# Expert values in halves with a bank each, and a token phase that begins with short spans

## The reference, cut to what matters

```python
logits = x_flat @ W_router
probs = jax.nn.softmax(logits, axis=-1)
topk_p, topk_i = jax.lax.top_k(probs, TOP_K)
topk_p = topk_p / topk_p.sum(axis=-1, keepdims=True)
...
for e in range(E):
    h = jax.nn.relu(x_flat @ W1[e] + b1[e])
    y = h @ W2[e] + b2[e]
    out = out + combine[:, e:e + 1] * y
```

## Time and profile before

| | us |
|---|---|
| median of 3 runs | 1411.34 |
| range of the runs | 1411.24 to 1416.61 |
| the profiled execution, its time | 1410.25 |
| its span, first to last instruction | 1408.4 |
| first row copy of the expert loop starts at | 448.7 |
| last row copy of the expert loop starts at | 942.2 |

### The profile page before, as it was taken

One profiled execution on the slowest core, in us unless ns is written; L12 is line 12 of the kernel. 1 busy time (PEld: TensorE's weight loads), 2 busy tenths in 40 slices (PEclk: granted clock), 3 DMA queues, 4 the chain that ended last, 5 costly groups with the idle time before them and its releaser, 6 DMA issues. The chain is left out here.

```text
span 1408.4 us, 32619 instructions
## 1 busy us (share of the span) xinstructions
PE 1103.4 (78%) x9950; PEld 731.9 (52%) x9951; DVE 825.5 (59%) x1640; ACT 744.3 (53%) x1748; POOL 546.3 (39%) x401
## 2 busy tenths in 40 slices
PE   6869787665602999999999989965999999965586
PEld 2324344332302988888888888862444444422354
DVE  3653345443525555555555555542899999984576
ACT  5855397655711555555555555544666666622364
POOL 0000006555570322322322222232799999991000
PEclk9989899888755999999999999998999999985599
DMA  6100001331122111111111111112111111101000
GB/s 202 47 1 0 1 1 54 112 129 52 33 67 62 44 39 37 38 38 37 37 38 38 38 37 37 38 31 82 30 30 60 60 60 60 46 30 77 0 1 30
DMA packets 60525, 65.22 MB, mean 46 GB/s; under 512 B 9841, under 2 KB 50301, under 8 KB 60336
## 3 DMA queue, kind: packets, MB, share of 16 engines
q1 hardware_dynamic: 49616, 46.47, 11.3%
q0 software_dynamic: 8832, 17.00, 3.7%
q10 hardware_dynamic: 2016, 0.94, 0.2%
HBM read 37.12 MB, written 28.55 MB: 47 GB/s over the span
## 5 line engine op out<-in xcount | busy, mean ns | idle before, releaser
L921 DVE SCALAR_TENSOR_TENSOR m_hl<-ps,m_hh 128x512 f16<-128x512 f32 x292 | 200.4, 686 | 158.2 <-ACT m_hh L893 155.9
L801 POOL DMA_INDIRECT expert_out<-m_result,m_token x148 | 144.5, 976 | 377.8 <-DVE m_result L933 374.1
L893 ACT ACTIVATE m_hh<-ps 128x512 f16<-128x512 f32 x292 | 174.2, 596 | 179.0 <-PE ps L854 176.7
L836 PE MATMUL ps<-m_x,weights 128*128 128x128 f16 x1168 | 212.8, 221 | 44.5 <-ACT m_x L887 43.7
L838 PE MATMUL ps<-m_x,weights 128*128 128x128 f16 x1168 | 211.7, 220 | 0.0
L837 PE MATMUL ps<-m_x,weights 128*128 128x128 f16 x1168 | 211.7, 220 | 0.0
L745 POOL DMA_INDIRECT dispatched<-d_rows,slot x128 | 128.4, 1003 | 211.6 <-DVE slot L647 126.2
L851 PE MATMUL ps<-weights,m_hh 128*128 128x128 f16 x1160 | 209.2, 219 | 0.0
L853 PE MATMUL ps<-weights,m_hl 128*128 128x128 f16 x1160 | 209.2, 219 | 0.0
L852 PE MATMUL ps<-weights,m_hh 128*128 128x128 f16 x1160 | 209.2, 219 | 0.0
L1043 POOL TENSOR_TENSOR iv_pool_sum<-iv_pool_sum,iv_pool_part 128x1024 f32<-128x1024 f32 x80 | 188.6, 2358 | 12.1 <-DVE iv_pool_part L1258 3.8
(11 more groups left out here) (306 smaller groups left out, 2238.0 us busy)
## 6 DMA issues: line engine op xcount, KB each, us to landing
m_rows<-dispatched SPq DMA_DIRECT2D x152, 65.5 KB
X<-x SPq DMA_DIRECT2D x16, 512.0 KB, 4.3
iv_got<-expert_out SPq DMA_DIRECT2D x16, 512.0 KB, 4.3
out<-X SPq DMA_DIRECT2D x16, 512.0 KB, 3.0
Y<-w_moe SPq DMA_DIRECT2D x8, 512.0 KB
expert_out<-m_result,m_token POOLq DMA_INDIRECT x148, 2.2
dispatched<-d_rows,slot POOLq DMA_INDIRECT x128
Y<-w_last SPq DMA_DIRECT2D x1, 2048.0 KB
```

What stands on the lines that cost most here:

```text
L801: pool.indirect_dma_start(env.yt, bass.IndirectOffsetOnAxis(ap=token[:, k:k + 1], axis=0), result[:, k, :], None, bounds_check=TOKENS - 1, ...
L836: pe.matmul(out, high, xh, start=True, stop=False)
L893: act.activation(hh[e][:, :], hidden[e], ACT.Relu).then_inc(hi_ready[e], 1)
L921: dve.scalar_tensor_tensor(hl[e][:, :], hidden[e], 0.0, hh[e][:, :], ALU.max, ALU.subtract).then_inc(h_split[e], 1)
```

## The change

In the expert phase:

- `hidden[e]` is two halves of 256 columns, and each half has a PSUM bank of its own; `y` and the two turned parts move to the other banks, so that all eight are used. `high` and `low` are issued for each half, with semaphore counts for each half. `high` of the first half waits only until `down` has read the first half of `hh` and `hl`.
- The turned rows are copied by two engines: ScalarE takes the high part, VectorE the low part (`xl_ready`). In `up` the two matmuls with the high part come first.
- VectorE's order is: low of expert 0's first half, copy of x's low part, low of expert 0's second half, both halves of expert 1, and only then token and result.

In the token phase:

- Spans have 2, 2, 2, 3, 3, 4, 4, 4, 4 and 4 units, so there are ten. A short span's `choose` and `pair` run in the first iteration after its last unit and `share` and `route` in the second; `ranks` runs both its parts in the second. Long spans keep their four iterations.
- The rows stand in one buffer of 12 units that is used as a ring, and `sent` has five semaphores.

One semaphore `passed`, which nothing waits on, takes the place of four. The span steps take only the columns of their span; these edits, which change only slices, are left out below.

```diff
-SPAN, ROW_SETS = 16, 3
-SPANS, SPAN_UNITS = TILES // SPAN, SPAN // UNIT_TILES
+SPAN_UNITS = (2, 2, 2, 3, 3, 4, 4, 4, 4, 4)
+SPANS, SPAN = len(SPAN_UNITS), max(SPAN_UNITS) * UNIT_TILES
+SPAN_FIRST = [sum(SPAN_UNITS[:c]) for c in range(SPANS)]
+SPAN_OF = [c for c in range(SPANS) for _ in range(SPAN_UNITS[c])]
+ROW_UNITS, SENT_SETS = 12, 5
...
-        rows = [sb(f"d0_rows{k}", [P, SPAN, ROW]) for k in range(ROW_SETS)]
+        rows = sb("d0_rows", [P, ROW_UNITS * UNIT_TILES, ROW])
...
         def rows_of(n):
-            first = n % SPAN_UNITS * UNIT_TILES
-            return halves[n // SPAN_UNITS % ROW_SETS][:, first:first + UNIT_TILES, :]
+            first = n % ROW_UNITS * UNIT_TILES
+            return halves[:, first:first + UNIT_TILES, :]
+
+        def tiles_in(c):
+            return SPAN_UNITS[c] * UNIT_TILES
+
+        def span_rows(c):
+            first = SPAN_FIRST[c] % ROW_UNITS * UNIT_TILES
+            return rows[:, first:first + tiles_in(c), :]
+
+        def slots_of(c):
+            return slice(SPAN_FIRST[c] * UNIT_TILES, SPAN_FIRST[c] * UNIT_TILES + tiles_in(c))
+
+        def sent_by(c):
+            return sum(tiles_in(k) for k in range(c % SENT_SETS, c + 1, SENT_SETS)) * 16
+
+        def rows_free(engine, c):
+            for n in range(SPAN_FIRST[c], SPAN_FIRST[c] + SPAN_UNITS[c]):
+                if n >= ROW_UNITS and (n == SPAN_FIRST[c] or SPAN_OF[n - ROW_UNITS] != SPAN_OF[n - 1 - ROW_UNITS]):
+                    earlier = SPAN_OF[n - ROW_UNITS]
+                    engine.wait_ge(sent[earlier % SENT_SETS], sent_by(earlier))
+
+        def step_at(n, long_step, short_step):
+            done = [c for c in range(SPANS) if SPAN_FIRST[c] + SPAN_UNITS[c] - 1 + (long_step if SPAN_UNITS[c] == 4 else short_step) == n]
+            return done[0] if done and done[0] < SPANS - 1 else None
...
             def ranks(c, part):
+                m = tiles_in(c)
                 if part == 0:
                     pe.wait_ge(summed, c + 1)
-                    pe.matmul(prefix, env.idf[:, :], seen[:, :].unsqueeze(1).broadcast_to([P, SPAN + 1, PAIRS]), start=True, stop=False)
+                    pe.matmul(prefix[:, 0:(m + 1) * PAIRS], env.idf[:, :], seen[:, :].unsqueeze(1).broadcast_to([P, m + 1, PAIRS]),
+                              start=True, stop=False)
                     pe.wait_ge(hot_ready, c + 1)
-                    pe.matmul(prefix[:, 0:SPAN * PAIRS], env.ltri[:, :], hot[:, :, :].rearrange("p t a -> p (t a)"), start=False, stop=False)
-                for t in range(0, 6) if part == 0 else range(6, SPAN):
-                    mm = pe.matmul(prefix[:, (t + 1) * PAIRS:(SPAN + 1) * PAIRS], env.ones16[:, :],
-                                   hot[:, t:t + 1, :].broadcast_to([P, SPAN - t, PAIRS]), start=False, stop=(t == SPAN - 1))
+                    pe.matmul(prefix[:, 0:m * PAIRS], env.ltri[:, :], hot[:, 0:m, :].rearrange("p t a -> p (t a)"), start=False, stop=False)
+                for t in range(0, 6) if part == 0 else range(6, m):
+                    mm = pe.matmul(prefix[:, (t + 1) * PAIRS:(m + 1) * PAIRS], env.ones16[:, :],
+                                   hot[:, t:t + 1, :].broadcast_to([P, m - t, PAIRS]), start=False, stop=(t == m - 1))
                 if part == 1:
                     mm.then_inc(prefix_ready, 1)
...
-                c, k = n // SPAN_UNITS - 1, n % SPAN_UNITS
-                if c >= 0 and k in (1, 2):
-                    ranks(c, k - 1)
+                for part, c in ((0, step_at(n, 2, 2)), (1, step_at(n, 3, 2))):
+                    if c is not None:
+                        ranks(c, part)
...
-                c = n // SPAN_UNITS
-                if n % SPAN_UNITS == 0:
-                    if c >= ROW_SETS:
-                        act.wait_ge(sent[c % ROW_SETS], c // ROW_SETS * SPAN * 16)
-                    act.activation(rows[c % ROW_SETS][:, :, C + 2], env.token_no[:, c * SPAN:(c + 1) * SPAN], ACT.Copy)
+                c = SPAN_OF[n]
+                if n == SPAN_FIRST[c]:
+                    rows_free(act, c)
+                    act.activation(span_rows(c)[:, :, C + 2], env.token_no[:, slots_of(c)], ACT.Copy)
...
+                c = step_at(n, 2, 2)
+                if c is not None:
+                    shares(c)
...
             def share(c):
+                w = views(c)[0]
                 dve.wait_ge(exp_ready, c + 1)
-                if c >= ROW_SETS:
-                    dve.wait_ge(sent[c % ROW_SETS], c // ROW_SETS * SPAN * 16)
-                tail = lambda g: rows[c % ROW_SETS][:, :, C + g]
-                link(dve.tensor_scalar(v["g1"], v["ex"], 1.0, WSCALE ** 2, ALU.add, ALU.mult))
...
-                c, k = n // SPAN_UNITS - 1, n % SPAN_UNITS
-                if c >= 0:
-                    if k == 0:
-                        choose(c)
-                    elif k == 1:
-                        pair(c)
-                    elif k == 2:
-                        share(c)
-                    else:
-                        route(c)
+                for step, long_step, short_step in ((choose, 1, 1), (pair, 2, 1), (share, 3, 2), (route, 4, 2)):
+                    c = step_at(n, long_step, short_step)
+                    if c is not None:
+                        step(c)
...
             for c in range(SPANS):
-                pool.wait_ge(normed, (c + 1) * SPAN_UNITS)
-                wait_apart(pool, routed, c + 1, env.passed["pool"])
-                for t in range(SPAN):
-                    at = c * SPAN + t
+                pool.wait_ge(normed, SPAN_FIRST[c] + SPAN_UNITS[c])
+                wait_apart(pool, routed, c + 1, env.passed)
+                for t in range(tiles_in(c)):
+                    at = SPAN_FIRST[c] * UNIT_TILES + t
                     pool.indirect_dma_start(env.xg, bass.IndirectOffsetOnAxis(ap=env.slot[:, at:at + 1], axis=0),
-                                            rows[c % ROW_SETS][:, t, :], None).then_inc(sent[c % ROW_SETS], 16)
-            for k in range(ROW_SETS):
-                pool.wait_ge(sent[k], len(range(k, SPANS, ROW_SETS)) * SPAN * 16)
+                                            span_rows(c)[:, t, :], None).then_inc(sent[c % SENT_SETS], 16)
+            for k in range(SENT_SETS):
+                pool.wait_ge(sent[k], sum(tiles_in(c) for c in range(k, SPANS, SENT_SETS)) * 16)
...
-        hidden = [env.psum[0][:, e * HALF:(e + 1) * HALF] for e in range(2)]
-        y = [env.psum[1][:, e * HALF:e * HALF + C] for e in range(2)]
-        turn = env.psum[2][:, 0:2 * P]
+        hidden = [[env.psum[e][:, h * HALF:h * HALF + H0 // 2] for h in range(2)] for e in range(2)]
+        y = [env.psum[2][:, e * HALF:e * HALF + C] for e in range(2)]
+        turn = [env.psum[3][:, k * HALF:k * HALF + P] for k in range(2)]
+        part_cols = [slice(h * H0 // 2, (h + 1) * H0 // 2) for h in range(2)]
...
             def turn_rows(i):
                 pe.wait_ge(rows_ready, i + 1)
                 pe.wait_ge(x_ready, i + 1)
+                pe.wait_ge(xl_ready, i + 1)
                 for part_ in range(2):
-                    mm = pe.matmul(turn[:, part_ * P:(part_ + 1) * P],
+                    mm = pe.matmul(turn[part_],
                                    halves[:, at(i), part_ * C:(part_ + 1) * C].rearrange("p k c -> p (k c)"), idh[:, :], start=True, stop=True)
                 mm.then_inc(turned, 1)
 
             def up(i, e, expert):
                 w = W[:, expert * WCOLS:(expert + 1) * WCOLS]
                 pe.wait_ge(x_ready, i + 2)
-                pe.wait_ge(h_split[e], i + 1)
                 for m in range(KM):
-                    out = hidden[e][:, m * P:(m + 1) * P]
+                    if m % 2 == 0:
+                        pe.wait_ge(h_split[e], i * 2 + m // 2 + 1)
+                    out = hidden[e][m // 2][:, m % 2 * P:(m % 2 + 1) * P]
                     high, low = w[:, m * P:(m + 1) * P], w[:, H0 + m * P:H0 + (m + 1) * P]
                     pe.matmul(out, high, xh, start=True, stop=False)
-                    pe.matmul(out, high, xl, start=False, stop=False)
-                    mm = pe.matmul(out, low, xh, start=False, stop=True)
-                mm.then_inc(h_ready[e], 1)
+                    pe.matmul(out, low, xh, start=False, stop=False)
+                    if m == 0:
+                        pe.wait_ge(xl_ready, i + 2)
+                    mm = pe.matmul(out, high, xl, start=False, stop=True)
+                    if m % 2 == 1:
+                        mm.then_inc(h_ready[e], 1)
 
             def down(i, e, expert):
                 w = W[:, expert * WCOLS:(expert + 1) * WCOLS]
-                pe.wait_ge(h_split[e], i + 2)
+                pe.wait_ge(h_split[e], i * 2 + 4)
                 if e == 0:
                     pe.wait_ge(part_ready, i + 1)
                 else:
                     high, low = w[:, 2 * H0 + k * P:2 * H0 + (k + 1) * P], w[:, 3 * H0 + k * P:3 * H0 + (k + 1) * P]
```

(66 more changed lines are left out.)

95 lines of the change are left out of this document (52 added, 43 removed).

## The result

The changed kernel takes 1352.05 us (median of 4, 1347.11 to 1355.87) against 1411.29 (1410.61 to 1416.61): ratio 0.957, 95% interval 0.953 to 0.961. Forecast was 1340. The profiled execution took 1350.42, its span is 1348.5.

What follows compares the result with a forecast made beforehand. The prediction took TensorE, with a 0.47 us hole a tile at the x copy, to bound the expert loop and no engine the token stage. 1410.25 - 61 (loop) - 10 (token stage) = 1339, put at 1340 as median; range 1312 to 1374.

Steps and rivals of the forecast that it cites:

- What bounds the kernel: Expert loop: TensorE, 52 matmuls at 0.056 us, 2.91 a tile, plus a 0.47 hole at the x copy; token stage: no engine.
- Copy of x: Expert loop: split over ScalarE (0.28 us) and VectorE (0.29), the copy lets TensorE restart at 2.85, so its wait goes.
- Halves: Expert loop: value halves take 0.383 us on ScalarE, 0.46 on VectorE; VectorE's 2.63 a tile stays under TensorE's 2.91.
- the hold: Expert loop: a TensorE completion falling right behind the end of a GpSimd scatter comes about 0.4 us late.
- Order of the waits: Expert loop: lows ahead of the result put the scatter's end 0.5 us into a tile, moving the hold off the path.
- New waits: TensorE's queue in the expert loop: five more waits cost 0.05 us a tile, making 2.96 and -61 us in all.
- Token stage: Shorter first spans bring the sixth span's slots to 290 instead of 300.1: -10 us, ends -33 and +12.
- (d): Expert loop: the scatter still ends where an awaited completion is due, tile 3.38, no change in the loop: 1401; chance 0.03.
- (b): Token stage: short bursts don't stop TensorE at all, -61 - 33: 1317; chance 0.12.
- (c): The token stage grows, as scatters and the stops with them begin earlier, -61 + 12: 1362; chance 0.09.
- (e): Expert loop, L921's successor: halves cost as much as wholes on VectorE, tile 3.55, slower at 1426; chance 0.04.
- (a): Expert loop: tile stays near 3.15, low(0)'s second half behind the x copy or new waits emptying TensorE's queue: 1367; chance 0.20.

Runs made afterwards that it cites:

- e8: Changed kernel with x copied by ScalarE alone, no copy on VectorE: ratio 0.954 to the kernel before, loop 445.4 us.
- e7: Changed kernel with the two low halves of the second expert behind the result: ratio 0.993 to the kernel before, loop 501.0 us.
- e9: Changed kernel with values read whole and VectorE's x copy ahead of both lows: ratio 1.009 to the kernel before, loop 516.9 us.
- e3: Changed kernel with the result's scatter left out of the expert loop, its semaphore incremented instead: loop 432.1 us, total not read.
- e5: Changed kernel with eight more GpSimd semaphore increments ahead of each result scatter: ratio 0.949 to the kernel before, loop 436.2 us.
- e11: Changed kernel with token spans of 2, 2, 2, eight times 3, and 2 units: ratio 0.951 to the kernel before, loop 453.0 us.
- e4: Changed kernel with two more GpSimd semaphore increments ahead of each result scatter: ratio 0.951 to the kernel before, loop 437.9 us.

## Why the prediction was right, and where it was off

*What bounds the kernel.* Right. TensorE's hole went, and its 0.056 a matmul stands: 2.90 a steady tile for 2.91.

*Copy of x.* Durations right (0.275 and 0.289 for 0.28 and 0.29), its wait gone. That the split of the copy is what removes the wait is not borne out: e8 has the same steady tile with the copy at 0.385. What removed it is the order, as e7 shows, where the wait is back.

*Halves.* 0.422 for my 0.46, ScalarE's 0.383 as put; VectorE's sum is 4 x 0.422 + 0.289 + 0.154 + 0.351 = 2.48 for 2.63. The Trainium skill, "VectorE: DVE Perf Modes", section "The TRN2 errata", makes an estimated 0.39; measured is 0.422, between it and my line. Its advice to keep pieces at 512 elements or more, for the fixed cost that each instruction pays, did not pay here: e9 obeys it and is 5% slower than the change, though part of that is the place of its x copy and the hold.

*Order of the waits.* "So the hold moves off the path" is the step that was off. The scatter ended about where I put it (0.5 in the tile; measured 0.6 to 0.7), and behind its end nothing awaited falls. But I had the hold begin at the scatter's end, from the one completion in the earlier trace rows that falls there. By the trace's semaphore records it begins some 0.55 us behind its start, so it also took down(1)'s completion. The shares of the 442.2: 146 x 2.903 = 423.8; 13 word stops x 0.37 = 4.8; 0.7 for the first two tiles; and 13 that go with the scatter (e3's loop, less the 2.5 us by which its start was slower, is 429.6).

*New waits.* I allowed 0.05 a tile, 7 us. They cost nothing (2.90); the word stops, which I had not seen, happen to take the same place. Had the hold been off the path the loop would have been 429.6 for my 432. Of the 12 us by which the forecast was low 10 are the loop's (442.2 for 432), and the hold's 13 more than cover them; 1 is the token stage, and the median lies 1.6 above the profiled execution where I took 1.1. So the forecast is near for a sound reason (the hole at the x copy) and by some luck: 7 us were put down for waits that cost nothing, and 5 of them were used up by word stops.

*Token stage.* -9.1 for -10. First slots near 194 were measured as a first scatter at 193.5, the sixth span's slots (put at 290) and ScalarE's stop behind its burst of 16 are:

```profile
291.51 0.17 DVE L684 SCALAR_TENSOR_TENSOR slot<-r_pid,r_rank 128x16 uint32<-128x16 f32 x1
...
315.13 0.28 ACT L554 ACTIVATE t_sq<-ps 128x128 f32<-128x128 f32 x1 [12.85 <-remote]
```

and the last scatter is at 417.0 for 415.

*Rivals.* (d) was true in kind for 24 of the 146 tiles, at a price of 13 us and not 61. (b) was wrong: bursts of 12 stop ScalarE too, if less. (c) was wrong: the token stage shrank by 9.1. (e) in the form "halves as costly as wholes" was wrong by the 0.422; a kernel slower than before is what e9 shows, for other reasons. (a) had 3.15 a tile; measured is 3.03, and not for its reason: the steady tile has no hole at the seventh matmul. The chances have a slip: (d) at 1401 would still be 10 us faster, more than the 7 named, so "all but (d) and (e)" should leave out (e) alone.

## What to carry to other kernels

An engine off the critical path can still decide its length by when it starts something: here 0.07 us in a GpSimd scatter's start made 0.55 us of a tile, of which the next tile gave back 0.11. Look in the trace at which completions fall into such an instruction, and move it with the order of the work around it. Undo the parts of a change one at a time: here the loop without the one (+8 us on the kernel before) and without the other (+23, with the x copy moved too) is slower than if neither had been made, and both together win 51. And see that undoing a part moves nothing else, or the price is that of both.

## What the runs showed of the hardware

- While GpSimd works on an indirect DMA, completions of TensorE reach the other engines late: those due from about 0.55 us after its start until some 0.35 behind its end are delivered 0.3 to 0.5 us after its end, most of them 0.35 to 0.42. ScalarE's and VectorE's own completions are on time where a waiting engine shows it: in the kernel before VectorE starts 0.03 us behind ScalarE's values 122 times with a scatter 0.7 to 0.9 us under way, and in e9's rows TensorE starts 0.06 behind VectorE's piece that ended 0.68 into a scatter. Where the held part begins isn't settled: 0.52 was on time and 0.56 held in the changed kernel, in e5 some at 0.25 were held, in the kernel before 0.7 was on time. The Trainium skill, "Perfetto Trace Analysis", section "DMA Instruction — SWDGE (GPSIMD)", says that the record of such a DMA ends when its last descriptor is written, not when the data has moved. That agrees with a hold that follows the record's end by about 0.4, but no run here shows which part of the chip does the holding.
- Behind bursts ScalarE stops for longer: 3 to 5 us with 12 scatters in a row, 10 to 13 with 16 (e11's rows, and the row of the changed kernel at 315.13), though only 6.5 to 7.5 in the first burst of 16. That this is the same hold is a reading; the profile names no releaser there.
- The first tiles of the loop come behind a stretch of over 20 us in which TensorE did nothing, and they begin at the lower clock level (1.2 GHz). In e3 it was there for a whole tile, which took 4.98 us (columns as in the earlier trace rows):

```profile
447.00:451.90 4.90, 4.57 (x42) 4.31 (x43) 1.06 (x4) 1.30 (x6) 0.00 (x0) 0.50 0.18 41
451.90:460.00 8.10, 8.10 (x138) 8.10 (x137) 6.19 (x18) 5.30 (x15) 0.00 (x0) 0.93 0.10 26
```

In the changed kernel, where the second tile took 3.09, it went up earlier (the granted clock is 0.97 from 443.0 to 446.1). In the changed kernel, e3, e4 and e5 the first three tiles take 0.7 to 3.2 us more than three steady ones.
